# Splitting the third chunk of the down weights per tile on GpSimd, from the third tile on

## What is computed

```python
x = x + xattn(layernorm(x), ctx)
h = layernorm(x)
topk_w, topk_idx = top_k(softmax(h @ gate.T), 2)
gu = einsum('th,efh->tef', h, gate_up)             # 8 experts, 2F = 704, H = 512
act = silu(gu[..., :F]) * gu[..., F:]              # F = 352
y = einsum('tef,te,ehf->th', act, combine, down)   # down: 352 -> 512 for each expert
y = y + shared_expert(h)
x = x + y
```

## Time and profile before

| | us |
|---|---|
| median of 3 runs | 348.38 (347.9 to 348.44) |
| the profiled execution's own time | 348.8 |
| its span, first to last instruction | 347.0 |
| PE busy | 330.1 (95%) |
| DVE busy | 274.1 (79%) |
| ACT busy | 235.4 (68%) |
| POOL busy | 121.7 (35%) |

### The profile page before, as it was taken

The page is one execution under the profiler, slowest core; times in us unless marked ns, Lnnn a source line. Parts: engine busy times, 40 slices in busy tenths (PEclk is TensorE's granted clock), DMA queues, the critical chain, the costliest instruction groups (busy, mean ns, idle before and its releaser), DMA issues.

```text
span 347.0 us, 6841 instructions
## 1 busy us (share of the span) xinstructions
PE 330.1 (95%) x2301; PEld 282.8 (81%) x2301; DVE 274.1 (79%) x477; ACT 235.4 (68%) x588; POOL 121.7 (35%) x130
## 2 busy tenths in 40 slices
PE   8999999999999999999999899999999999999990
PEld 7898876777776787889898789899889889898880
DVE  5888988999956358855487999999999989889920
ACT  4666989999974232212326588988898889889730
POOL 4332752555551000164400007746732221321321
PEclk9999999999999999999999999999999999999996
DMA  7999200000002799993689944554464556356343
GB/s 242 374 345 379 89 3 2 3 2 0 3 3 66 302 357 346 421 338 134 216 264 220 318 160 87 113 130 82 94 134 100 89 106 133 83 92 135 51 48 43
DMA packets 31793, 53.00 MB, mean 153 GB/s; under 512 B 7440, under 2 KB 14992, under 8 KB 30736
## 3 DMA queue, kind: packets, MB, share of 16 engines
q1 hardware_dynamic: 27616, 43.34, 38.5%
q0 software_dynamic: 4144, 9.23, 14.6%
HBM read 32.22 MB, written 16.92 MB: 142 GB/s over the span
## 4 chain that ended last, share of the span: by engine, by line
PE 61%; ACT 15%; DVE 9%; DMA 7%; issue 4%; POOL 1%; POOLq 1%; SPq 0%; DVEq 0%; ACTq 0%
PE bank L549 24%; PE bank L867 20%; ACT prob L1028 10%; PE bank L891 4%; DMA out<-y_sb,dest 3%; DMA act_w<-act_e 2%; PE bank L905 2%; PE bank L895 2%; PE bank L766 2%; DVE gu_parts L1264 2%; PE bank L734 2%; ACT probT L983 2%; PE bank L901 1%; PE bank L941 1%; PE bank L541 1%
## 5 line engine op out<-in xcount | busy, mean ns | idle before, releaser
L528 POOL DMA_INDIRECT out<-y_sb,dest x21 | 38.3, 1826 | 115.6 <-DMA out<-y_sb,dest 64.0
L1264 DVE TENSOR_TENSOR gu_parts<-w_gu,gu_parts 128x704 fp32r<-128x704 f32 x84 | 76.3, 943 | 0.2
L983 ACT ACTIVATE gu_parts<-w_gu 128x704 fp32r x84 | 66.4, 794 | 13.1 <-PE bank L867 11.5
L867 PE MATMUL bank<-gu_parts,xsT_hi 128*128 128x352 f32 x328 | 69.8, 334 | 1.4 <-DVE xsT_lo L1264 1.0
L867 PEld LDWEIGHTS bank<-gu_parts,xsT_hi 128*128 128x128 f32 x328 | 53.7, 188 | 8.7 <-issue 8.5
L867 PE MATMUL bank<-gu_parts,xsT_lo 128*128 128x352 f32 x164 | 39.7, 323 | 0.0
L549 PE MATMUL bank<-x2T_hi,w_sg_lo 128*128 128x512 f32 (+1 forms) x88 | 32.6, 370 | 0.2
L549 PE MATMUL bank<-x2T_hi,w_sg_hi 128*128 128x512 f32 (+1 forms) x88 | 32.0, 363 | 0.0
L549 PE MATMUL bank<-x2T_lo,w_sg_hi 128*128 128x512 f32 (+1 forms) x88 | 32.0, 363 | 0.0
L867 PEld LDWEIGHTS bank<-gu_parts,xsT_lo 128*128 128x128 f32 x164 | 28.6, 189 | 0.0
L983 ACT ACTIVATE act_s_hi<-act_s 128x512 fp32r<-128x512 f32 (+1 forms) x10 | 5.8, 578 | 32.5 <-DVE act_s L1450 24.3
(11 more groups left out here) (219 smaller groups left out, 837.0 us busy)
## 6 DMA issues: line engine op xcount, KB each, us to landing
w_gu<-guT SPq DMA_DIRECT2D x8, 1408.0 KB, 9.7
xs_dram<-no_row SPq DMA_DIRECT2D x1, 5460.0 KB, 19.8
xs_in<-xs_dram SPq DMA_DIRECT2D x21, 256.0 KB, 4.6
w_dn<-dnT SPq DMA_DIRECT2D x8, 512.0 KB, 5.5
act_w<-act_e SPq DMA_DIRECT2D x19, 176.0 KB, 2.8
w_sg<-sguT SPq DMA_DIRECT2D x10, 256.0 KB, 5.4
w_dn<-dnT SPq DMA_DIRECT2D x8, 192.0 KB, 6.5
w_sd<-sdnT SPq DMA_DIRECT2D x5, 256.0 KB, 4.9
```

Of the source, the lines that this page charges most:

```text
L528: pool.indirect_dma_start(out=out[:, :], out_offset=bass.IndirectOffsetOnAxis(ap=dest[:, i, 0:1], axis=0), in_=y_sb[i % 2][:, :], in_offse ...
L867: ins = pe.matmul(dst[:, 0:F], xsT[x_][:, c, :], gu2[w_][:, c, f0:f0 + F], start=c == 0 and n == 0, stop=c == C - 1 and n == 2)
L983: act.activation(dst, src, ACT.Copy).then_inc(s[sem], 1)
L1264: dve.tensor_tensor(lo_, src, hi_.bitcast(F32), ALU.subtract).then_inc(s[sem], 1)
```

## The change

From tile 2 on (`SPLIT_FROM = 2`) every down product takes its third chunk in the split form. `dn_last` no longer holds one split for each expert but two pairs of buffers of one chunk each. GpSimd splits for each tile: behind scatter i it reads the expert of tile i+2 from `eid` and splits that expert's third chunk into pair (i+2) % 2, for tiles 2 to 20, 19 times instead of 7. PE waits for the split of its tile, addresses `dn_last` statically, and reads no expert number for these tiles.

```diff
-    SPLIT_FROM = 9
-    assert SPLIT_FROM * P >= T
+    SPLIT_FROM = 2
...
+    last_at = [xres_at, xres_at + 4 * NX * H]
+    dn_last = [tuple(m.inside(last_at, f"dn_last{k}_{part}", [P, H], F32R) for part in ("hi", "lo")) for k in range(2)]
...
-            def split_dn_last(e):
+            def split_dn_last(i):
+
                 k, w = FK[2]
-                src = w_dn[0:w, e * DN + 2 * H:(e + 1) * DN]
-                hi_, lo_ = (t[0:w, (e - 1) * H:e * H] for t in dn_last)
+                e = pool.value_load(eid[0:1, i:i + 1], min_val=0, max_val=E - 1)
+                src = w_dn[0:w, bass.ds(e * DN + 2 * H, H)]
+                hi_, lo_ = (t[0:w, :] for t in dn_last[i % 2])
                 pool.tensor_copy(hi_, src).then_inc(s["dn_last_hi"], 1)
-                pool.wait_ge(s["dn_last_hi"], e)
+                pool.wait_ge(s["dn_last_hi"], i - SPLIT_FROM + 1)
                 pool.tensor_tensor(lo_, src, hi_.bitcast(F32), ALU.subtract).then_inc(s["dn_last"], 1)
...
-                if i < E - 1:
-                    split_dn_last(i + 1)
+                if i + SPLIT_FROM < NT:
+                    split_dn_last(i + SPLIT_FROM)
...
-            def down(i, e, split=False):
+            def down(i, e=None):
+                split = e is None
...
                 if split:
+                    pe.wait_ge(s["dn_last"], i - SPLIT_FROM + 1)
                     for n, (x_, w_) in enumerate(((1, 0), (0, 1), (0, 0))):
-                        ins = pe.matmul(A[:, :], actT_last[x_][0:w, :], dn_last[w_][0:w, bass.ds(e * H - H, H)],
+                        ins = pe.matmul(A[:, :], actT_last[x_][0:w, :], dn_last[i % 2][w_][0:w, :],
                                         start=False, stop=n == 2)
...
-                e = expert(i - 1, lowest=int(i > SPLIT_FROM))
+                e = expert(i - 1) if i <= SPLIT_FROM else None
...
-                if i == NT - 2:
-                    e_last = [expert(n, lowest=1) for n in (NT - 2, NT - 1)]
...
-                if i == SPLIT_FROM + 1:
-                    pe.wait_ge(s["dn_last"], E - 1)
-                down(i - 1, e, split=i > SPLIT_FROM)
+                down(i - 1, e)
```

More of the change, by code:

```diff
@@ L906, in down, with last_down @@
                               start=False, stop=True).then_inc(s["edn"], 1)
-            def last_down(i, e):
+            def last_down(i):
                 k3, w3 = FK[2]
@@ L911, in last_down @@
                 w_of = lambda part, at, width: [dn2[part][:, k, at:at + width] for k in range(2)] + \
-                    [dn_last[part][0:w3, bass.ds(e * H + (at - H), width)]]
+                    [dn_last[i % 2][part][0:w3, at:at + width]]
                 pe.wait_ge(s["dn_hi"], i + 1)
                 pe.wait_ge(s["dn_lo"], i + 1)
+                pe.wait_ge(s["dn_last"], i - SPLIT_FROM + 1)
                 pe.wait_ge(s["aT_hi"], i + 1)
@@ L970, in _ @@
             pe.wait_ge(s["ey"], NT - 2)
-            down(NT - 2, e_last[0], split=True)
+            down(NT - 2)
             last_gate_then_up(range(C // 2, C))
@@ L976, in _ @@
             pe.wait_ge(s["sres"], NX * ND)
-            last_down(NT - 1, e_last[1])
+            last_down(NT - 1)
         @block.scalar
```

## The result

| | before | changed |
|---|---|---|
| median | 348.38 us (11 runs, 346.97 to 349.14) | 349.84 us (11 runs, 348.65 to 351.53) |
| profiled execution: own time, span | 348.8, 347.0 | 349.33, 347.5 |
| DVE busy | 274.1 (79%) | 282.4 (81%) |
| POOL busy | 121.7 (35%) | 154.9 (45%) |
| `act_e` of tile 2 to `act_e` of tile 19 | 114.64 | 326.19 - 211.24 = 114.95 |

The ratio is 1.0047, with a 95% interval of 1.003 to 1.0064: slower by half a percent. All ratios in this document leave out slow executions; there is one, of nosub (351.85 us), and its median leaves it out too. The forecast was 349.9 us. That it is so close is partly luck, as "Why the prediction came out as it did" shows: the bound did pass to where DVE never waits, but not for the reason that was given.

The account below looks back on a forecast made before the run. The bound was to pass from PE to DVE at 6.82 us a tile: +1.30 for 17 tiles, +0.4 late landings, -0.2 tail, +1.5 us in all; forecast 349.9 us, 8-in-10 range 347.5 to 352.6.

Parts of the forecast that it names:

- That splits and the extra operation never met before: Expert loop: before the change, seven early tiles pay for POOL's split, only later ones have `actT_last_lo`; afterwards every tile has both.
- the extra operation: DVE's `actT_last_lo` in the expert loop: 0.28 us, 0.19 net of overlap, added in seven intervals from tile 3 on.
- DVE's sum: DVE per tile: 6.04 own work, 0.65 to 0.84 lost to POOL, 0.03 handoff; 6.72 to 6.91 us, above PE's 6.64.
- the ring: Not forecast, from the experiments: POOL's copy waits for DVE's `gu_parts` subtraction, POOL's subtraction delays DVE's next; 3.18 + 3.59 us.
- The rule weighed: Skill's rule for VectorE and GpSimd on SBUF: first to start keeps the port, other fully blocks; forecast said the trace disagrees.
- half speed: DVE's `gu_parts` pair beside POOL's copy: 1.35 us taken for 0.70 us of work, a loss of 0.65.
- Rival B: First to start keeps the port: DVE loses only 0.32 us, 6.36 a tile, PE stays the bound, 347.8 us; chance 0.05.
- Rival A: PE remains the bound if POOL's copy runs in about 612 ns: DVE 6.54 us a tile, 347.8 us; chance 0.18.
- Rival C: POOL's split starts earlier, sliding over DVE's whole `gu_parts` pair: tile of 7.02 us, some 353.3 us; chance 0.17.
- Where PE waits: Late tiles: PE idle 0.1 to 0.2 us before the first chunk, released by `xsT_lo`, behind `act_e` in DVE's queue.
- The sum: Expert loop: 17 x 6.82 = 115.94 against 114.64, +1.30; plus 0.4 late landings, less 0.2 tail: +1.5 us.
- 0.4 for late landings: Late landings of `act_w` in the expert loop: 0.39 us each with DVE as bound, none to two; 0.4 taken.

Follow-up runs that it names:

- nosub: Changed kernel without POOL's subtraction behind its third and later copies: median 348.81 us, ratio 1.0025 to the kernel before, tiles 6.64 us.
- nolast: Changed kernel without DVE's operation `actT_last_lo` for tiles 2 to 19: median 349.55 us, ratio 1.0033 to the kernel before, tiles 6.77 us.
- twice: Changed kernel with DVE's operation `actT_last_lo` made twice for tiles 2 to 20: median 351.08 us, ratio 1.008 to the kernel before, tiles 6.77 us.
- nopool: Changed kernel with POOL's splits only behind the first two scatters: median 348.43 us, ratio 0.9991 to the kernel before, tiles 6.64 us, five of 6.9 to 7.4.
- phase: Changed kernel with POOL waiting for DVE's second `gu_parts` subtraction ahead of the expert-number load: median 360.31 us, ratio 1.0341 to the kernel before.
- phase2: Changed kernel with POOL waiting for DVE's second `gu_parts` subtraction between expert-number load and copy: 348.6 us, ratio 1.0015 to the kernel before; repeated, 347.34 us, 0.9996.

## Why the prediction came out as it did

**That splits and the extra operation never met before** was true, and that tiles from 9 on would pay for the split, was right: 6.77 us instead of 6.64.

**DVE's sum** was the wrong frame. The prediction put DVE's own work, the extra operation and the loss in a line: 6.04 + 0.65 to 0.84 + 0.03 = 6.72 to 6.91, middle 6.82. The losses were sized well: 0.65 and 0.22, as rows of 2.33 and 1.90 against 1.68 show. DVE's own part was 0.14 too high: a tile of 6.77 less 0.65 and 0.22 leaves 5.90 and not 6.04, since without waits the rows overlap more (`act_e` starts 0.20 us after `actT_last_lo`, which takes 0.27). That 5.90 + 0.87 gives the tile exactly is no proof of the sum, since that holds for any tile in which DVE never waits. And nolast and twice show that the extra operation (0.19 in the sum) is no term of the bound, and nopool and nosub that the bound needs both of POOL's operations. The bound is the ring, 3.18 + 3.59 = 6.77. It stood in the trace of before already: a copy at 242.61 and the next at 249.38 are 6.77 apart, while `act_e` went from 244.38 to 251.09, 6.71. The ring was slower than PE by some hundredths, and the first pair grew tile by tile, from 1.68 through 1.72, 1.75, 1.78, 1.82 and 1.87 to 1.91; seven splits were too few for that to use up DVE's slack. I read the growing pair as a size to be averaged and not as a drift between two clocks.

**The rule weighed.** I took the trace to disagree with the Trainium skill (SBUF — State Buffer, "Who interferes with whom"), and half of that reading falls. By the rule one of the two engines "fully blocks", and phase agrees, with a copy of 3.84 us beside subtractions at full speed. My half speed then was an average over taking turns; that is the reading that fits both rows, and nothing measures it inside the 1.53 us. That the first to start goes on is not borne out by the recorded starts: in the trace of before DVE's second operation is recorded 0.18 us before the copy and is held up, and in phase the copy is recorded 0.58 us before the pair (239.97 against 240.55) and is passed. So a recorded start need not be the moment that decides; the copy's start is tied to the end of DVE's first operation, with 0.10 between. Rival B, which I built on the rule, was wrong all the same, because it let DVE's second operation keep the port by its recorded start.

**Rival A** fell with its condition: the copy of the new form takes 1.80 us, like the old one.

**Rival C** (the split slides over the pair) did not come: the scatters start 1.16 to 1.65 us before their copies in the changed kernel, and the copy stays at 0.96 to 1.00 from the pair's start. Its place is set by DVE and not by the scatter, as long as the scatter is early enough. Its warning was sound, though: phase moved the copy by force and got 7.41 us, at another place and in another way.

**Where PE waits** was named wrong (`xsT_lo`; it was `actT_last_lo`), and the 0.1 to 0.2 us of idle time in PE's own row did not show, only waits of its weight loads. Neither changes a number of the forecast.

**The sum.** 17 x 6.82 = 115.94 was 0.99 above the 114.95 that the trace shows, and the 0.4 for late landings was not there in any of four traces. So for the profiled execution I was 1.4 us too high in the loop. In all it was 1.0 (350.3 against 349.33), since the stretch began 0.49 us later than before, which the change doesn't explain. The median hit because it doesn't follow the profiled pair: the trace of before holds two late landings, 1.14 us, and its execution is above its median; without them its stretch would be 113.5, and 115.0 against that is +1.5. I added a late landing after, and should have taken two away before; that 0.4 and the 0.85 from a tile 0.05 too long happened to make up for them. That the medians' +1.46 equals this +1.5 is an account that fits, not something shown: of the changed kernel's 17 executions without a trace 11 are above the slowest traced one (the traced ones took 348.69 to 350.07), up to 353.09, and no trace shows one of these. What they lose, and where, stays open.

**What the change costs** is then: 10 intervals (from `act_e` of tile 9 on) at 6.77 instead of 6.64, 1.3 us, and 7 at 6.70 to 6.78 instead of 6.71 to 6.74, 0.2 us. The PE work that it saves, 0.56 us, is lost because PE doesn't bound these tiles; phase2, where it does, has them at 6.64.

## What to carry to other kernels

When two engines share something, look for the order in which they take it before adding up what each loses: a distance that repeats to a hundredth of a microsecond, while what seems to trigger it varies by tenths, is a ring, and work outside it is free until the room beside it is used up (here about 0.4 us of PSUM reads, from nolast to twice). To see whether an operation is a term of the bound, take it away and then make it twice; two cheap runs said more here than the sum did. And place GpSimd's SBUF work beside VectorE operations that read PSUM, with a semaphore and everything slow (the load of an index) ahead of the wait: the copy went from 1.80 to 0.60 us, and VectorE lost nothing. Against the kernel before, the times of the whole kernel show no gain from it.

## What the runs showed of the hardware

- A GpSimd copy of 96 x 512 took 0.60 us when it met no two-input VectorE subtraction and no scatter in progress, 1.80 behind a scatter and beside a subtraction, 1.17 to 1.20 behind a scatter with VectorE idle (the last copy of the changed kernel, at 331.16) or reading PSUM (nosub, at 289.56), and 3.84 when it came too late (phase). The 612 ns of the other copy are thus near what this one takes undisturbed.
- Beside such a split the subtraction of 128 x 704 loses 0.65 us. In the changed kernel that is the time from the end of the first operation of the pair (242.16 + 0.88 = 243.04) to the end of the scatter's own row (241.68 + 2.01 = 243.69). A scatter without a copy behind it costs VectorE nothing (nopool), and a copy beside PSUM reads neither (phase2; nosub at 289.56, behind a scatter). Whether the scatter or the copy behind it holds VectorE up in those 0.65 us was not tried.
- A waiting copy doesn't get in between every two back-to-back two-input operations of VectorE: in phase three of them passed it. Why it gets in between the two of one pair in the changed kernel and not there is open.
